# Attention scores multiplied twice: once for the row maximum, once transposed with shift and mask in PSUM

## The reference

```python
h = tok(x)                       # weights over the 4 groups from a small MLP and a softmax -> (16, 128, 256)
h = h + attn(layernorm(h))
h = h + moe(layernorm(h))        # 64 experts, 6 per token, and a shared expert

# attn: 16 heads of 16, 128 tokens per image
scores = einsum('bqhd,bkhd->bhqk', Q, K)
scores = where(causal, scores, -inf)
probs = softmax(scores / sqrt(hd), axis=-1)
out = einsum('bkhd,bhqk->bqhd', V, probs).reshape(B, S, H) @ W_o.T + b_o
```

## Time and profile before

| what | us |
|---|---|
| median of 3 runs | 524.37 (523.19 to 525.21) |
| span of the profiled execution | 527.1 |
| busy: TensorE / weight loads / VectorE | 463.1 / 351.2 / 331.5 |
| busy: ScalarE / GpSimd | 278.4 / 244.1 |
| attention pipeline, steps 3 to 15 | 92 to 245 of the span |
| expert tiles | about 283 to 480 |

### The profile page before, as it was taken

One profiled execution on the slowest core, in us unless ns is written; L12 is line 12 of the kernel. 1 busy time (PEld: TensorE's weight loads), 2 busy tenths in 40 slices (PEclk: granted clock), 3 DMA queues, 4 the chain that ended last, 5 costly groups with the idle time before them and its releaser, 6 DMA issues. The chain is left out here.

```text
span 527.1 us, 11459 instructions
## 1 busy us (share of the span) xinstructions
PE 463.1 (88%) x2974; PEld 351.2 (67%) x2974; DVE 331.5 (63%) x1065; ACT 278.4 (53%) x902; POOL 244.1 (46%) x273
## 2 busy tenths in 40 slices
PE   1687989999999999987648999999999999996796
PEld 1556666766666776755225888888888888873564
DVE  4682658998999999888661443444444444440897
ACT  3285778888777888873201444444445544440000
POOL 1111110566555666666770565665655665661000
PEclk9996989999999999998776999999999999998899
DMA  8999930111111111112224559667678566652997
GB/s 275 348 347 309 299 99 2 61 63 60 62 63 61 62 62 61 63 70 81 101 100 114 181 171 291 203 188 241 200 209 270 165 209 212 205 157 65 415 390 282
DMA packets 56471, 89.82 MB, mean 170 GB/s; under 512 B 7719, under 2 KB 43690, under 8 KB 56400
## 3 DMA queue, kind: packets, MB, share of 16 engines
q1 hardware_dynamic: 44016, 61.62, 37.5%
q0 software_dynamic: 10080, 25.29, 13.6%
q10 hardware_dynamic: 2304, 2.10, 1.1%
HBM read 83.93 MB, written 40.82 MB: 237 GB/s over the span
## 5 line engine op out<-in xcount | busy, mean ns | idle before, releaser
L419 POOL DMA_INDIRECT y_rows<-y,xring x114 | 112.1, 984 | 90.8 <-issue 82.8
L1048 PE MATMUL ps<-wring,prob 128*128 x456 | 119.7, 386 | 0.0
L1009 DVE TENSOR_TENSOR probt<-probt,ps 128x128 f32<-128x128 f32 x114 | 32.8, 288 | 108.6 <-issue 90.7
L1048 PEld LDWEIGHTS ps<-wring,prob 128*128 128x128 f32 x456 | 79.4, 194 | 6.3
L474 ACT ACTIVATE prob<-ps,nmax 128x128 f32<-128x128 f32 x256 | 69.7, 391 | 4.1 <-DVE nmax L706 3.3
L572 ACT COPY prob<-ps 128x256 f32<-128x256 f32 x115 | 42.8, 372 | 48.6 <-PE ps L1279 48.3
L1048 PE MATMUL ps<-wring,probt 128*128 x228 | 68.2, 381 | 0.0
L577 ACT ACTIVATE probt<-ps 128x128 f32<-128x128 f32 x114 | 31.6, 277 | 58.3 <-PE ps L1048 58.3
L1002 DVE TENSOR_SCALAR y<-ps,xring 128x256 f32<-128x256 f32 x114 | 54.6, 479 | 5.8 <-DMA y_rows<-y,xring 4.6
L389 POOL DMA_INDIRECT slot_rows<-row,slot_ix x48 | 50.7, 1056 | 13.7 <-issue 13.4
L389 POOL DMA_INDIRECT slot_rows<-xring,slot_ix x48 | 50.4, 1050 | 14.0 <-issue 13.7
(11 more groups left out here) (173 smaller groups left out, 790.2 us busy)
## 6 DMA issues: line engine op xcount, KB each, us to landing
wring<-wexp SPq DMA_DIRECT2D x115, 384.0 KB
xring<-slot_rows SPq DMA_DIRECT2D x115, 129.0 KB, 2.3
x_sb<-y_rows SPq DMA_DIRECT2D x16, 768.0 KB, 6.3
slot_rows<-pads SPq DMA_DIRECT2D x1, 8256.0 KB, 33.9
x_sb<-x SPq DMA_DIRECT2D x3, 2048.0 KB, 17.8
slot_rows<-pads SPq DMA_DIRECT2D x5, 516.0 KB, 9.6
x_sb<-x SPq DMA_DIRECT2D x4, 512.0 KB, 5.1
out<-h_all ACTq DMA_DIRECT2D x16, 128.0 KB, 6.6
```

What stands on the lines that cost most here:

```text
L419: nc.gpsimd.indirect_dma_start(out=y_dram, out_offset=bass.IndirectOffsetOnAxis(ap=xring[:, q, TO_AT:TO_AT + 1].bitcast(I32), axis=0), in_ ...
L1009: nc.vector.tensor_tensor(hm[:, t % 2, :], silu[:, t % 2, :], psS[t % 2][:, INTER:2 * INTER], ALU.mult).then_inc(S("h_ready"), 1)
L1048: return nc.tensor.matmul(*a, **k)
```

## The change

The scores of an image are now multiplied twice, and both products lie in the image's own step.

1. `scores()`: all four groups, query rows, for the maximum alone. The mask is no longer written by one 512-column product per group, but added after the product by four products per group on 32x32 tiles, each with the columns from its diagonal on (512, 384, 256 and 128 columns).
2. `nmax_of(b, half)`: one reduction over two banks. `shift_of` splits the negated maximum into two bf16 parts in `shift_b`.
3. `turn_shift()`: one product with the identity turns the shifts; ScalarE copies them to `shift_t`.
4. `keyed()`: the product again with keys as weights and queries moving, so that rows are keys, head by head; to it are added the shift (a product of `pick_b` and `shift_t`) and the transposed mask in 32x32 tiles, all in PSUM.
5. ScalarE `exp(g)`: one 512-wide exponential per group without a bias, straight into `probt`, which has four places now. The transposes of the probabilities and their copies are gone.

The order in the queues is new too: ScalarE's sums stand at the top of the step, its copies follow in another order, the queries come last; VectorE alternates placing, routing and mixing; on TensorE all four value products stand at the end of the step.

```diff
+                def exp(g):
+                    act.wait_ge(S("keyed_done"), b + 1)
+                    wait(act, S("pv_done"), NGRP * (b - 1) + g + 1)
+                    nc.scalar.activation(probt[:, g].rearrange("p a k -> p (a k)"), psQ[g][:], ACT.Exp).then_inc(
+                        S("exp_done"), 1)
...
+            def nmax_of(b, half):
+                dve.wait_ge(S("scores_done"), b + 1)
+                two = slice(2 * half, 2 * half + 2)
+                nc.vector.tensor_reduce(nmax[:, two, :], ps_low[:, two, :].rearrange("p g (a k) -> p g a k", a=GH),
+                                        axis=AX, op=ALU.max, negate=True).then_inc(S("shift_parts"), 1)
+
+            def shift_of(b, part):
+
+                dve.wait_ge(S("shift_parts"), 3 * b + 2 + part)
+                if part == 0:
+                    wait(dve, S("shift_turned"), b)
+                    nc.vector.tensor_copy(shift_b[:, :, 0:GH], nmax[:]).then_inc(S("shift_parts"), 1)
+                else:
+                    nc.vector.tensor_tensor(shift_b[:, :, GH:2 * GH], nmax[:], shift_b[:, :, 0:GH],
+                                            ALU.subtract).then_inc(S("shift_ready"), 1)
...
                 if has(b):
-                    nmax_of(b, 2)
-                    nmax_of(b, 3)
-                if has(a):
-                    mix(a, 0)
+                    nmax_of(b, 0)
                 if has(cc):
                     den_of(cc)
...
+                mixed(0)
+                placed(0)
...
+                if has(cc):
+                    normalise(cc)
+                if has(b):
+                    nmax_of(b, 1)
+                placed(1)
+                if has(b):
+                    shift_of(b, 0)
+                placed(2)
+                if has(b):
+                    shift_of(b, 1)
+                mixed(1)
+                placed(3)
+                placed(4)
+                mixed(2)
+                routed(0)
+                placed(5)
+                routed(1)
+                mixed(3)
...
+                routed(2)
...
+                placed(6)
+                routed(3)
...
+                def scores():
+
+                    pe.wait_ge(S("k_ready"), 2 * b + 2)
+                    pe.wait_ge(S("q_ready"), 2 * b + 2)
+                    wait(pe, S("exp_done"), NGRP * b)
                     for m in range(2):
...
+                        for g in range(NGRP):
+                            at = 32 * g
+                            mm(psQ[g][:, m * 2 * P:(m + 1) * 2 * P], qt[at:at + 32, par, m, :],
+                               kpair[at:at + 32, par, m, :, :].rearrange("p a k -> p (a k)"),
+                               start=m == 0, stop=False)
+                    for r in range(4):
+                        for g in range(NGRP):
+                            at, n = 32 * g, P - 32 * r
+                            last = mm(psQ[g][32 * r:32 * r + 32, :].rearrange("p (a k) -> p a k", a=GH)[:, :, 32 * r:P],
+                                      ident_b[at:at + 32, at:at + 32],
+                                      tri_b[at:at + 32, 0:n].unsqueeze(1).to_broadcast([32, GH, n]),
+                                      start=False, stop=True)
+                    last.then_inc(S("scores_done"), 1)
+
+                def turn_shift():
+
+                    pe.wait_ge(S("shift_ready"), b + 1)
+                    wait(pe, S("ot_ready"), b)
+                    mm(psO[:, 0:P], shift_b[:].rearrange("p g n -> p (g n)"), ident_b[:], start=True,
+                       stop=True).then_inc(S("shift_turned"), 1)
+
+                def keyed():
+
+                    pe.wait_ge(S("shift_copied"), b + 1)
                     for j in range(GH):
...
+                        m, half = j // 2, j % 2
+                        for g in range(NGRP):
+                            at = 32 * g
+                            mm(psQ[g][:, j * P:(j + 1) * P], kpair[at:at + 32, par, m, half, :],
+                               qt[at:at + 32, par, m, :], start=j == 0, stop=False)
+                    for j in range(GH):
+                        for g in range(NGRP):
+                            at = 32 * g
+                            mm(psQ[g][:, j * P:(j + 1) * P], pick_b[at:at + 32, j, :], shift_t[at:at + 32, :],
+                               start=False, stop=False)
+                    for r in range(3, -1, -1):
+                        for g in range(NGRP):
+                            at, n = 32 * g, 32 * r + 32
+                            last = mm(psQ[g][32 * r:32 * r + 32, :].rearrange("p (a k) -> p a k", a=GH)[:, :, 0:n],
+                                      ident_b[at:at + 32, at:at + 32],
+                                      tri_tb[at:at + 32, P - n:P].unsqueeze(1).to_broadcast([32, GH, n]),
+                                      start=False, stop=True)
+                    last.then_inc(S("keyed_done"), 1)
```

More of the change, by code:

```diff
@@ L53 @@
 C_AT = {}
-for _name, _n in (("ident", P), ("causal", P), ("before", P), ("half", 2), ("ebase", E),
+for _name, _n in (("ident", P), ("tri", P), ("tri_t", P), ("pick", GH), ("before", P), ("half", 2), ("ebase", E),
                   ("dest", NB * TOPK), ("spill", 1 + NY), ("upto", E), ("tile", NTAB)):
@@ L496, in queries @@
                                          bias=bq_small[:, m:m + 1], scale=HD ** -0.5).then_inc(S("q_ready"), 1)
-                if has(b):
-                    turn(0)
-                    turn(1)
+                for img in ACT_SUMS.get(b, ()):
+                    sum_image(img)
+                if b > 1 and b - 1 in PART_AT:
+                    mixing_exp(PART_AT[b - 1])
                 if has(v):
@@ L534, in step @@
                 if has(b):
-                    turn(2)
-                    turn(3)
-                if has(v):
-                    exp(v, 0)
-                    exp(v, 1)
+                    act.wait_ge(S("shift_turned"), b + 1)
+                    wait(act, S("keyed_done"), b)
+                    nc.scalar.copy(shift_t[:], psO[:, 0:P]).then_inc(S("shift_copied"), 1)
+                    for g in range(NGRP):
+                        exp(g)
                 if has(a):
@@ L552, in step @@
                     nc.scalar.copy(ot_sb[:].rearrange("p a k -> p (a k)"), psO[:]).then_inc(S("ot_ready"), 1)
+                if has(a):
+                    for m in range(2):
+                        queries(m)
                 if b in PART_AT:
@@ L1168, in step @@
                     last.then_inc(S("ot_turned"), 1)
-                if has(v):
-                    pe.wait_ge(S("q_ready"), 2 * v + 2)
-                    both(psA[:, 0:D], lambda k: xnt[:, q, k, :], lambda k: wqkv_sb[:, k, 2 * D:3 * D]).then_inc(
-                        S("v_done"), 1)
                 if has(e):
                     pe.wait_ge(S("sel_ready"), e + 1)
+                    wait(pe, S("counted"), e)
                     if b in PART_AT:
@@ L1188, in step @@
                     two(psX, row_of(d)[:, 0, :], "x2_transposed")
-                if has(b):
-                    pv(1)
+                if has(a):
+                    pe.wait_ge(S("ln1_done"), a + 1)
+                    wait(pe, S("v_ready"), a)
+                    two(psA, xn[:, par, :], "xn_transposed")
                 if has(cc):
@@ L1198, in step @@
                     two(psC, o_sb, "o_transposed")
-                if has(a):
-                    pe.wait_ge(S("ln1_done"), a + 1)
-                    wait(pe, S("v_ready"), a)
-                    two(psA, xn[:, par, :], "xn_transposed")
                 shared_between(b, 1)
@@ L1208, in step @@
                     mixing_in(2)
-                if has(v):
-                    scores(v, 0, q)
                 if has(d):
```

194 lines of the change are left out of this document (70 added, 124 removed).

## The result

| | before | changed |
|---|---|---|
| median of 4 runs, us | 524.79 | 504.96 |
| lowest to highest, us | 523.19 to 529.04 | 504.11 to 508.44 |
| span of the profiled execution, us | 527.1 | 502.3 |
| VectorE's 1536-wide row of step 3, us | 92.17 | 80.39 |
| the same row of step 15, us | 244.87 | 219.75 |

The ratio is 0.961, 95% interval 0.957 to 0.966: 19.8 us less. Predicted were 510 us, within 503 to 522.

What follows compares the result with a forecast made beforehand. VectorE, 92% busy in the attention pipeline, was taken as the bound. Steps 4 to 15 falling from 152.7 to 138.9 us (-13.8) and the start's -1 made -14.8: 510 us, range 503 to 522.

Steps and rivals of the forecast that it cites:

- the chain: Serial work of one image within a step, from scores through maxima, second product and exponentials to last value product: 11.0 us.
- VectorE's loop: VectorE's own work per step in the attention middle: from 12.68 to 11.3 us, bounds 11.0 and 12.3.
- The near tie: Attention steps: serial work of 11.0 us against VectorE's 11.3; since they don't align, 11.6 us per step was taken.
- Four row groups: TensorE's score product: sixteen records in 1.13 us if four groups overlap; rival that they don't, 8%, 535 us.
- The 0.5 us a step: TensorE, both products: by the skill page's 3.07 times for four row tiles, some 0.5 us a step longer.
- VectorE's order: VectorE alternating placing, routing and mixing separates about eight dependent pairs at 0.12 us each: -1.0 us a step.
- the end of the gate wait: VectorE's 0.47 us wait for ScalarE's tanh goes, as the first routing step now stands later: -0.45 us a step.
- a gain up to there is kept whole: Time gained up to the root of step 15 stays in the total; the 31.5 us of GpSimd scatters behind don't move.
- The clock: Rival, 20%: TensorE's gaps drop its clock to 1.2 GHz, +1.5 us a step; in half of twelve steps 519 us.
- 1.5 us for steps 7 to 9: Extra time left in these steps for VectorE's token-mixing work, which stays: 1.5 us.
- The start: Steps up to 3, waiting for tables, token mixing and slow clock: -1 us, between +2 and -5.
- the 518 us for a VectorE that keeps its step: Rival, 13%: separated pairs bring nothing, VectorE takes 12.3 us a step, gain only 6 us, so 518 us.

Runs made afterwards that it cites:

- the run with the row copies: Changed kernel, VectorE writing the normalised image once, not six times, and ScalarE copying it to the other five rows: ratio 0.953 to the kernel before, median 500.6 us.
- the one with sixteen exponentials: Changed kernel with sixteen exponentials of 128 columns in place of four of 512: ratio 0.973 to the kernel before.
- the second trace of before: The kernel before, unchanged, run and traced once more: ratio 1.000, span 524.6 us, step 3 ending at 89.62 us.

## Why the prediction was right, and where it was off

**The middle, steps 4 to 15: the bound was right, the sum in part by luck.** 139.4 us were measured and 138.9 forecast, but steps 4 to 9 took 74.2 in place of 71.1, steps 13 to 15 30.7 in place of 33.0 (9.4, 11.2 and 10.1, where the chain was to keep them at 10.6 to 11.3), and the two misses cancel. What sets steps 13 to 15 isn't traced. In the middle proper the step is 11.49 us against 11.6. VectorE's loop was forecast at 11.3 and is 11.49, full to 98%. This too hides two terms: beside GpSimd's bias addition, which the prediction had at nothing, it loses 0.55 us where it lost 0.2 before, and the rest of the loop fell by 1.5 in place of 1.4. The chain was summed to 11.0, and two runs put it at 11.15 to 11.3: adding 0.65 to it gave 11.8, and taking 0.66 from VectorE gave 11.3. By its parts: scores 1.15 and masks 0.39 (forecast 1.5 together), VectorE's part 3.7 from 178.55 to 182.28 (4.1), shift and output projection 1.2 (1.05), the second product 1.7 (1.9), exponentials 2.07 (2.1), values behind them 0.7 (0.3). The near tie was real: 0.2 to 0.35 us lie between the two loops. After such a change, work added on either side shows up: 0.60 us on VectorE made the step 0.8 longer (0.2 of it beside the bias addition), 0.65 and 0.76 on the chain made it 0.3 and 0.2 longer.

**Four row groups: right.** Sixteen records in four groups take 1.15 us, eight in two groups took 1.13. The Trainium skill's 3.07 times (TensorE: Matmul & The Clock Gate, Part 3) for four tiles over one isn't tested as such, since no run has a single row group; four do twice the work of two in the same time. The 0.5 us a step that I had estimated from that page didn't come, and there the measurement decides.

**VectorE's order: right in size, incomplete in its condition.** I had priced it at -1.0 and the end of the gate wait at -0.45 as two terms. Undone, it cost 0.8 to 1.2 a step; put alone into the old kernel it cost 1.5 more. It pays only because ScalarE's exponentials no longer stand ahead of the tanh. The prediction said of ScalarE's 4.1 us that they have "no value by itself"; they were what made the order possible.

**ScalarE right, GpSimd in part.** ScalarE is busy 18.42 us in three steps, 6.1 each (forecast 6), and waits 2.47 for the second product. GpSimd waits 4.0 us for the variance in steps 10 to 12, 1.3 each as forecast, but 18.0 in the nine steps from which the forecast came, 2.0 each. The stretch behind step 15 kept its length (282.2 and 282.6 us), though its 24 scatters take 32.9 us in place of 31.5; over the traces that have the 1536-wide row it lies between 281.3 and 286.4, so "a gain up to there is kept whole" holds for this pair and not to the microsecond.

**The clock: the rival came true once, not in half of the steps.** One stretch of 3.4 us in step 7. Its cost lies between 0.6 and 2.5 us in steps 7 to 9: these take 38.4 us, against 35.3 in the run with the row copies (less the 0.2 a step by which that one is shorter) and 37.8 in the one with sixteen exponentials, both at the full clock there. I had left 1.5 us for steps 7 to 9; they took 3.9 more than three middle steps.

**The start: the term that was mis-sized.** It was taken as -1, with bounds from +2 to -5, and is -9.2. The failed step is "I take -1", and the bounds themselves: I drew them from steps 2 and 3 alone and left out steps -1 to 1, where 5.8 of the 9.2 us lie (mark of step 1 at 61.4 in the second trace of before, 55.61 after). The runs say this much: before has 6.8 us at half clock between 45 and 53, after 3.4; more TensorE work on the chain moved the mark of step 3 by 7.6 us, with 6.8 more at half clock, and that is more than twice what it did in twelve steps of the middle; the tanh of step 0 moved forward brought 2.6, with 3.4 less at half clock. This fits a serial start, partly at half clock, in which what the change takes off the chain counts in full or more. No run isolates it, and how the 9.2 us split isn't settled.

**The sum.** By the spans of the first traces the forecast was 512.3 us and the result is 502.3: the start gave 10.8 more than forecast (11.8 for 1), the middle 0.5 less, and 0.3 more stand behind step 15. By the medians the miss is only 5 us, which puts the result 2 us inside the range's low end: that the start's miss didn't carry it out is luck. The profiled execution of before was a long one for its kernel, about 528.9 us if it lies as far above its span as that of after (504.11 to 502.3), which is 4 above the median; that of after is the fastest of its four. One slip in the prediction's rivals: the 518 us for a VectorE that keeps its step leaves out the start's -1.

## What to carry to other kernels

Reordering independent short chains on a full engine is worth its gaps only if nothing that the new order asks for earlier is late. Test an order in the kernel in which it will run, since alone it can cost more than it brings.

When two loops tie, price both: add a known cost to each in turn and see how much reaches the step. Here that told 11.5 from 11.2 us, and that moving 0.66 us to an idle engine would be worth 0.2 a step and no more.

Price the start by its own rows, all of its steps, and at the clock that it has. A long wait next to a long step isn't its cause until it is gone and the step is shorter: two such waits were moved here, and the step stayed long.

A full engine may be full with instructions that take longer than they need. Compare an instruction's time with its like in other steps, and look at what the neighbouring engines do when it is long: here 0.55 us of an 11.49 us step showed only in this way.

## What the hardware showed beside this

- An exponential of 128 columns with its bias per partition takes 0.27 us of pitch (eight in 2.17), without it 0.18 (sixteen in 2.83). That was the error in the run with sixteen. The Trainium skill (ScalarE: Activation LUTs, "What ACT_TABLE_LOAD costs") gives some 93 ns for each such operand; by that page, the trace agrees.
- Sixteen masks of 32 by 32 in bf16, up to 512 columns, take 0.39 us, and 64 take 1.04: 0.22 for each further sixteen.
